# The second sequence's first attention in two passes, its last tile apart; sums of the second attention on GpSimd

## The reference

```python
# x (2, 512, 128), ctx (2, 77, 128)
x = x + tanh(g_xattn[0]) * attn0(ctx, layernorm(x))    # queries from x, keys and values from [ctx-norm, x-norm]: 512 + 77 = 589; 8 heads of 64
x = x + tanh(g_ffn[0])   * ffn0(layernorm(x))          # quantised 128 -> 512, depthwise conv of 3 along the tokens, silu, quantised 512 -> 128
x = x + tanh(g_xattn[1]) * attn1(layernorm(x), ctx)    # 16 heads of 8, 77 keys, rotary positions
x = x + tanh(g_ffn[1])   * moe(layernorm(x))           # 8 experts of 64, the two best weighted, and a shared one

def attn0(...):                 # per head
    sim = q @ k.T               # logits are large, so q and k are each split into an upper and a lower part
    p = exp(sim - max(sim)); out = (p @ v) / sum(p)
def ffn0(x):                    # act_quant: round(x * 127 / max|x|) over a token's row
    h = bit_linear(x, w1); h = conv1d(h, 3 taps, padding 1); return bit_linear(silu(h), w2)
```

## Time and profile before

| | |
|---|---|
| runs | 273.53, 274.93, 277.11 us |
| profiled execution | 273.79 us, of which the span 271.9 us |
| TensorE clock granted over the whole span | 1.0 of full speed (2.4 GHz) |
| busy: TensorE, its weight loads | 248.7, 183.7 us |
| busy: VectorE, ScalarE, GpSimd | 230.7, 184.0, 32.3 us |
| turn of the last first-attention probabilities | about 165 us |
| start of the last subtraction of the second attention (L1175) | 236.8 us |

### The profile page before, as it was taken

One profiled execution on the slowest core, in us unless ns is written; L12 is line 12 of the kernel. 1 busy time (PEld: TensorE's weight loads), 2 busy tenths in 40 slices (PEclk: granted clock), 3 DMA queues, 4 the chain that ended last, 5 costly groups with the idle time before them and its releaser, 6 DMA issues.

```text
span 271.9 us, 5419 instructions
## 1 busy us (share of the span) xinstructions
PE 248.7 (91%) x1754; PEld 183.7 (68%) x1754; DVE 230.7 (85%) x561; ACT 184.0 (68%) x462; POOL 32.3 (12%) x57
## 2 busy tenths in 40 slices
PE   0999999999999999999999999968868899899996
PEld 0757687787688866677678878745545565657665
DVE  5699969886679976999989789899999999998781
ACT  2596668776577557868879862159799596773561
POOL 3100000000001010000000021320002302133230
PEclk9999999999999999999999999999999999999999
DMA  6198620030300003300300000000000000000001
GB/s 203 38 251 298 159 58 2 0 91 0 91 0 1 4 0 89 91 0 4 89 0 4 0 2 0 4 0 0 1 2 2 2 0 4 0 10 4 29 0 41
DMA packets 8848, 10.70 MB, mean 39 GB/s; under 512 B 1115, under 2 KB 5877, under 8 KB 8821
## 3 DMA queue, kind: packets, MB, share of 16 engines
q1 hardware_dynamic: 7792, 9.70, 13.4%
q10 hardware_dynamic: 1029, 0.65, 0.8%
HBM read 4.99 MB, written 0.52 MB: 20 GB/s over the span
## 4 chain that ended last, share of the span: by engine, by line
PE 62%; DVE 23%; issue 7%; ACT 6%; DMA 1%; DVEq 0%; ACTq 0%
PE slot L535 18%; PE slot L621 11%; PE slot L602 6%; PE slot L603 5%; PE slot L580 3%; PE slot L762 3%; PE slot L628 2%; PE slot L586 2%; DVE nm L1063 2%; ACT S L916 2%; DVE mx L1172 2%; ACT PR L842 2%; PE slot L756 2%; PE slot L592 1%; PE slot L713 1%
## 5 line engine op out<-in xcount | busy, mean ns | idle before, releaser
L842 ACT ACTIVATE PR<-slot,nm 128x589 f32<-128x589 f32 x64 | 47.5, 749 | 14.7 <-DVE nm L1063 12.5
L1063 DVE TENSOR_REDUCE nm<-slot 128x1 f32<-128x589 f32 x64 | 46.4, 763 | 3.7 <-PE slot L603 3.2
L535 PE MATMUL slot<-K,PR 128*128 128x128 f32 (+1 forms) x320 | 44.4, 278 | 1.6 <-ACT PR L842 1.5
L535 PEld LDWEIGHTS slot<-K,PR 128*128 128x128 f32 (+1 forms) x320 | 35.5, 142 | 12.3 <-ACT PR L842 9.6
L602 PE MATMUL slot<-KH,Q 128*128 128x296 f32 (+1 forms) x128 | 40.7, 336 | 0.8 <-DVE PT L779 0.4
L621 PE MATMUL slot<-PT,V 128*64 128x256 f32 (+1 forms) x320 | 38.1, 384 | 0.0
L603 PE MATMUL slot<-KL,Q 128*128 128x296 f32 (+1 forms) x128 | 36.2, 299 | 0.0
L621 PEld LDWEIGHTS slot<-PT,V 128*64 128x64 f32 (+1 forms) x320 | 21.6, 137 | 11.9 <-issue 2.7
L602 PEld LDWEIGHTS slot<-KH,Q 128*128 128x128 f32 x128 | 24.1, 189 | 5.5 <-issue 2.1
L777 ACT ACTIVATE PT<-slot 128x640 f32<-128x640 f32 x34 | 23.5, 704 | 6.5 <-PE slot L535 5.8
L779 DVE COPY PT<-slot 128x640 f32<-128x640 f32 x30 | 24.4, 820 | 2.7 <-PE slot L535 2.3
(11 more groups left out here) (170 smaller groups left out, 500.8 us busy)
## 6 DMA issues: line engine op xcount, KB each, us to landing
KH<-KH SPq DMA_DIRECT2D x16, 147.5 KB, 2.5
KL<-KL SPq DMA_DIRECT2D x16, 147.5 KB, 2.5
CTT<-in_ctxT SPq DMA_DIRECT2D x1, 640.0 KB, 7.8
K<-in_const SPq DMA_DIRECT2D x1, 589.0 KB, 8.8
WGU<-in_wgu SPq DMA_DIRECT2D x1, 580.0 KB, 8.6
out<-X SPq DMA_DIRECT2D x8, 64.0 KB, 1.5
L1W<-in_l1w SPq DMA_DIRECT2D x1, 384.0 KB, 3.6
WD<-in_wdT SPq DMA_DIRECT2D x1, 320.0 KB, 11.3
```

What stands on the lines that cost most here:

```text
L535: return pe.transpose(dst, src, ident[0:p, 0:p])
L842: act.activation(PR[:, s, :], W[:, K0:K0 + KEYS0], ACT.Exp, bias=nm0[:, s:s + 1], accum_out=sum0[:, b, p * 2 + f, t, e:e + 1]).then_inc(pr ...
L1063: dve.tensor_reduce(nm0[:, s:s + 1], W[:, K0:K0 + KEYS0], AX.X, ALU.max, negate=True).then_inc(max_ready, 1)
```

## The change

`PLAN` is another string: all engines have a new order from the first word on. Beside it:

- The `u` and `w` items of the second sequence are made in two passes over the four head pairs (`PASSES`). The first pass takes tiles 0, 1 and 2; within a head pair the `w` of tiles 0 and 1 is 256 tokens wide, that of tile 2 is 128. The second pass takes tile 3 alone, with a `w` of 128 tokens for each pair. So there are 12 `w` items in place of 8, and 8 `q` items (384 and 128 tokens wide) in place of 4 (512).
- `KH` and `KL` have room for all four head pairs, since the second pass reads them again.
- Norm and quantisation of the second sequence's tiles go as (0, 1), (2), (3) in place of (0, 1), (2, 3); `f1` as (0, 1, 2), (3).
- `f2` of the second sequence is made in two halves of 256 tokens (each with two more input columns, 258): eight items in place of four.
- The sum over the 77 keys for heads 8 to 15 moves from VectorE to GpSimd: one `tensor_reduce` becomes seven additions that halve the row each time (`add_up`, stage `P3`), each waiting for the one before.
- To make room, `PT1` and `HM` have fewer buffers (`PT1` one, `HM` two), the scratch tiles `RC` and `RK` are gone (their role is played by the PSUM slot), and the shared expert's product stays in `SHT`.
- Of the 64 `u` copies, VectorE makes 22 in place of 30, ScalarE 42 in place of 34. Idle transposes: 56 in place of 68.

```diff
+PASSES = [(((0, 1), (2, 3)),), (((0, 1), (2,)), ((3,),))]
+NORMED = [((0, 1), (2, 3)), ((0, 1), (2,), (3,))]
+TURNED = [((0, 1, 2, 3),), ((0, 1, 2), (3,))]
+CHUNKS = [(((0, S), (0, S)),), (((0, N), (0, N + 2)), ((N, S), (N - 2, S)))]
+KSLOT = [0, 1, 2, 3] * B
+KSLOTS = 4
...
-        out += [("u", b, p, f, t, e) for p in range(NP0) for f in range(2) for t in range(TP) for e in range(2)]
...
+        for groups in PASSES[b]:
+            for p in range(NP0):
+                out += [("u", b, p, t, e) for g in groups for t in g for e in range(2)] + [("w", b, p, g) for g in groups]
...
 PLAN = """
-x0:F0 x0:A1 k:F2+8@2 x0:D2 q:F4 k:A1 k:F0 q:A1 k:D1 v:F6 x0:P2 k:A1 q:D1 v:F2 v:Ca k:D1 q:F5 v:Ca u:F6 x0:D3
...
+x0:F0 x0:A1 k:F2+8@2 x0:D2 q:F4 k:A1 v:F0 q:A1 k:D1 x0:P2 k:F6 v:Ca q:D1 k:F2 k:A1 k:F0 x0:D3 k:A1 v:F4 k:D1
...
-        KH = sb("KH", [P, 4, KEVEN], F32R)
-        KL = sb("KL", [P, 4, KEVEN], F32R)
+        KH = sb("KH", [P, 2 * KSLOTS, KEVEN], F32R)
+        KL = sb("KL", [P, 2 * KSLOTS, KEVEN], F32R)
...
-        PT1 = sb("PT1", [P, 2, 2 * KC1, N])
+        PT1 = sb("PT1", [P, 2 * KC1, N])
...
+        FOLD = sb("FOLD", [P, HH, 32])
...
-        HM = sb("HM", [P, QT, MT])
+        HM = sb("HM", [P, 2, MH])
...
+            def add_up(item):
+
+                def fold(out, x, y):
+                    folds[0] += 1
+                    pool.tensor_tensor(out, x, y, ALU.add).then_inc(pool_step, 1)
+                    pool.wait_ge(pool_step, folds[0])
+
                 n = upto(item)
...
+                s, m = (n - 1) % RING, item[1] * QT + item[2]
+                pool.wait_ge(exp1_ready, HH * n)
+                x = S1[:, s, 0:HH * C].rearrange("p (h c) -> p h c", c=C)
+                if n > 2:
+                    pool.wait_ge(sum1_added, n // 2 - 1)
+                fold(FOLD[:], x[:, :, 0:32], x[:, :, 32:64])
+                fold(FOLD[:, :, 0:C - 64], FOLD[:, :, 0:C - 64], x[:, :, 64:C])
+                for w in (16, 8, 4, 2):
+                    fold(FOLD[:, :, 0:w], FOLD[:, :, 0:w], FOLD[:, :, w:2 * w])
+                pool.tensor_tensor(sum1[:, m, HH:H1].unsqueeze(2), FOLD[:, :, 0:1], FOLD[:, :, 1:2],
+                                   ALU.add).then_inc(sum1_added, 1)
...
-                elif kind == "a4":
-
-                    m, s = item[1] * QT + item[2], (n - 1) % RING
-                    dve.wait_ge(exp1_ready, HH * n)
-                    dve.tensor_reduce(sum1[:, m, HH:H1], S1[:, s, 0:HH * C].rearrange("p (h c) -> p h c", c=C),
-                                      AX.X, ALU.add).then_inc(sum1_added, 1)
```

More of the change, by code:

```diff
@@ L89, in upto, with pass_of, queries, chunk_of @@
     return PLACE[item]
+def pass_of(b, t):
+    return next(i for i, groups in enumerate(PASSES[b]) if any(t in g for g in groups))
+def queries(b, i):
+    return PASSES[b][i][0][0] * P, (PASSES[b][i][-1][-1] + 1) * P
+def chunk_of(b, t):
+    return next(ch for ch, ((lo, hi), _) in enumerate(CHUNKS[b]) if lo <= t * P < hi)
+def readers_of_queries(item):
+    _, b, i, p = item
+    return [x for x in KINDS["u"] if x[1:3] == (b, p) and pass_of(b, x[3]) == i]
+def readers_of_keys(g):
+    return [x for x in KINDS["u"] if x[1:3] == divmod(g, NP0)]
 def wide(item):
@@ L417, in quantised, with keys @@
             return qb_copied[COPIES[item]], copied(item, COPIES[item])
-        def half_pair(item):
-            return (item[1] * NP0 + item[2]) * 2 + item[3]
+        def keys(g, e, rows=slice(0, P)):
+            n = 2 * KSLOT[g] + e
+            return KH[rows, n, :], KL[rows, n, :]
         def walk(engine, stages):
@@ L437, in double @@
             def double(g):
-                for part, signal in ((KH, k_upper), (KL, k_ready)):
+                for part, signal in ((0, k_upper), (1, k_ready)):
                     sp.wait_ge(signal, 2 * (g + 1))
@@ L639, in front @@
                 elif kind == "f1":
-                    mm = turn_tiles(W, b, 1)
+                    for j, t in enumerate(item[2]):
+                        pe.wait_ge(xn_ready[1], b * QT + t + 1)
+                        mm = turn(W[:, j * P:(j + 1) * P], XN[:, b * QT + t, :])
                 elif kind == "f2":
-                    c = item[2]
-                    pe.wait_ge(xqt_ready, b + 1)
+                    _, b, ch, c = item
+                    (_, hi), (first, after) = CHUNKS[b][ch]
+                    pe.wait_ge(xqt_ready, max(upto(x) for x in KINDS["f1"] if x[1] == b and x[2][0] * P < after))
                     pe.wait_ge(w1q_ready, 1)
-                    pe.matmul(W[:, 0:S], W1Q[:, c * P:(c + 1) * P], XH[:], start=True, stop=False)
-                    mm = pe.matmul(W[:, 0:S], W1Q[:, c * P:(c + 1) * P], XL[:], start=False, stop=True)
+                    for x in (XH, XL):
+                        mm = pe.matmul(W[:, 0:after - first], W1Q[:, c * P:(c + 1) * P], x[:, first:after],
+                                       start=x is XH, stop=x is XL)
                 elif kind == "f3":
@@ L768, in copy_turned @@
         def copy_turned(engine, by, item):
-            _, b, p, f, t, e = item
-            n, g = upto(item), half_pair(item)
+            _, b, p, t, e = item
+            n, w = upto(item), next(w for w in KINDS["w"] if w[1:3] == (b, p) and t in w[3])
+            g, at = upto(w) - 1, (t - w[3][0]) * P
             engine.wait_ge(prob_turned, n)
@@ L785, in copy_turned1 @@
             engine.wait_ge(p1_turned, n)
-            if part >= 2:
-                engine.wait_ge(front_done, NTH[KINDS["a6"][part - 2]] + 1)
-            dst = PT1[:, part % 2, h * KC1:(h + 1) * KC1, t % TP * P:(t % TP + 1) * P]
+            if part >= 1:
+                engine.wait_ge(front_done, NTH[KINDS["a6"][part - 1]] + 1)
+            dst = PT1[:, h * KC1:(h + 1) * KC1, t % TP * P:(t % TP + 1) * P]
             src = slot(item)[:, 0:KP1].rearrange("p (c q) -> p c q", c=KC1)
@@ L799, in copy_values @@
             if b == 1:
-                engine.wait_ge(front_done, NTH["w", 0, NP0 - 1, 1] + 1)
+                engine.wait_ge(front_done, NTH[[w for w in KINDS["w"] if w[1] == 0][-1]] + 1)
             rows, n = (P, 2) if j < 2 else (C, 1)
@@ L1080, in first @@
                     link(stats(1, X1, m))
[L1081 to L1082 removed]
+                    for x in KINDS["n"]:
+                        if x[1] == b and x[2][-1] == item[2]:
+                            variance(1, normed(x))
                 elif kind == "s":
```

311 lines of the change are left out of this document (172 added, 139 removed).

## The result

The changed kernel takes **278.59 us** (median of 20 runs, 275.6 to 282.8); the kernel before, on the same chip, 275.71 us (20 runs, 273.5 to 278.3). The ratio is 1.0094, interval [1.0062, 1.0125]: slower by about 0.9%. The forecast was 272.5 us, a little faster than before, so its direction is wrong. The profiled execution took 277.83 us, span 276.0. The ratio is not that of the two medians, since it leaves out executions that were over 1.5% slower than the fastest of their kernel.

What follows compares the result with a forecast made beforehand. TensorE was taken to bound A and C, VectorE B. Terms +0.5 - 2.6 - 1.9 + 1.5 + 0.8 = -1.7 us took the profiled 273.8 to 272.1; with the median 1.1 higher, forecast 272.5 us, range 265 to 280.

Steps and rivals of the forecast that it cites:

- A: Stretch from 16.9 to 165 us, until the first attention's last probabilities are turned; forecast to grow by 0.5 us.
- A, TensorE, +3.5 us: First attention: narrow `w`, one more `a3` and `o`, and norm transposes, less query work, add 3.5 us of TensorE work.
- What the lighter VectorE gives back: First attention: a third of the 8.9 us that TensorE's weight loads waited for exponentials comes back, -3.0 us.
- The two `k` that stand earlier: At the start: two `k` come earlier and the same two are missing later; keeping the keys costs TensorE nothing.
- B: Stretch from 165 to 237.5 us, until the second attention's last subtraction begins: VectorE -2.6, its idle time -1.9, GpSimd +1.5 us.
- C: Stretch from 237.5 us to the end, led by TensorE: more matmuls to issue, +0.8 us.
- holds by additions: Second attention: VectorE's SBUF-only steps are held until GpSimd's additions end, +1.5 us, ends 0 and 6.
- the worth of the sums: Second attention: seven of eight sums leave VectorE at 780 ns each, -5.5 us of instruction time, times 0.91 as busy time.
- The two signs of being wrong: Prediction is wrong if A moves over 4 us either way, or held VectorE steps sum to over 4 us.
- The pass is not what sets the time: Rival, no change: tile 3's attention covers only work that had cover before; 277.0 us, chance 0.18.
- GpSimd holds VectorE: Rival, slower: from the first `a4`, some 30 VectorE steps each meet an addition and wait; 282.6 us, chance 0.14.
- The tail balances: Rival, faster: first attention's waits vanish wholly or by two thirds, idle closes; 267 us, other form 268.7; chance 0.33.

## Why the prediction was wrong

- **A, TensorE, +3.5 us: right in size, half in effect.** Narrow products are 1.25 us. Summed from start to start by tile, the products grew by 2.0 us, their transposes by 0.5, `a3` by 1.6; what else came and left nearly cancels. But only a third to two thirds of such a sum shows in A.
- **"What the lighter VectorE gives back", -3.0 us: the step that failed.** A was to be 0.5 us longer and is 4.0. In size, VectorE lost 0.7 us of busy time in A, not 2.9: the copies in A took off 5.7 us for the 6.6 counted, and the rest of the count came out heavier. So against the kernel before there was hardly a lighter VectorE that could give anything back. In mechanism, the exchange itself did not pay either: taking 5.7 us from VectorE in the old order, and 6.3 more in the new, with ScalarE fuller by about as much, made A 1.8 us longer in the one and its second half 0.8 us longer in the other. The waits were read as slack in which one engine can be relieved; the round of scores, maximum, exponential, turn and copy passes through all three engines, and the copies went to the one whose exponentials the turns wait for. One run speaks for the term: putting eight copies back in the new order cost 3.3 us. There the move repaired what the new order had loaded on VectorE in the second half; it gained nothing over the kernel before.
- **The start, not priced.** The two `k` that stand earlier were named and costed at nothing. The first score came 1.2 us later in the profile. With the changed start order it was at 17.6 us or later in every profile, with two pairs' keys ahead or four; with the old one between 16.5 and 17.5. Which step of the start does it was not tried.
- **B and C: the sum fits better than its terms, by luck.** Forecast -3.0 and +0.8, measured -1.4 and +1.5, with the clock down for 10 us in them. The profiled 277.8 us stands 1 to 2 us above what the runs give at full clock; less those, B and C together are -1 to -2 against -2.2. Inside B two terms missed against each other: VectorE's busy time, holds included, fell by 3.1 us where -2.6 + 1.5 = -1.1 was forecast, and its idle time grew by 1.8 where it was to fall by 1.9. The holds by additions (1.4 us) and the worth of the sums (2.3 to 4 us against 3.5) fit. The holds by products were not priced. The two signs of being wrong that the prediction named both stand at their edge: A moved by 4.0 us, and all held steps in B and C come to 4.2 (1.4 before).
- **The rivals.** *The pass is not what sets the time* (277.0 us) comes closest in number: A kept its TensorE work and the sums paid for part of it; the profiled time is 277.8. Its reason, too little cover for tile 3, was not tested. *GpSimd holds VectorE* did not happen, its point of decision (20 steps held for 0.3 us) was not reached. For the old order the sums alone did cost 1.6%, by the route in C. *The tail balances* did not happen: no wait of A vanished.
- The Trainium skill, Perfetto Trace Analysis, "Identifying the Most-Contended Engine", takes weight-load busy and not matmul busy as TensorE's measure. In A of the kernel before loads were 77% busy and matmuls 98%, and TensorE's work counted in the length by a third to two thirds: neither share says that.
- The Trainium skill, GPSIMD Engine Reference, "Engine selection", gives reductions along the free dimension to VectorE. The old order agrees (1.0164 with the sums on GpSimd), the new one does not: 1.0239 with the sums on VectorE, 1.0094 on GpSimd.
- **What stays open.** A grew 2.8 us from first score to last turn; TensorE's rule of thumb gives 1.2 to 2.3 of it. The rest, and why the new order needs the eight copies on ScalarE to stay at that, was not taken apart further: debt of the first half and cost of the two passes stand together in it.

## What to carry to other kernels

A wait for an engine in the profile is not time that a lighter engine gives back: move one instruction's worth of load and time it before counting on it, above all where three engines hand each block round. Cut a stretch where the work changes before adding up an engine's load; a total over 150 us hid that VectorE got lighter in one half and heavier in the other. Test a shift of load in both directions: here fewer copies on VectorE gained nothing, and more cost 3.3 us. And a stretch that got shorter after reordering may have lent its work to its neighbours; compare what was done in it, not only its length.
